# Order of the opening loads, and where the attention gate is computed, in an adaLN block with attention-like mixing and a lookup-table FFN

## What is computed

```python
mod = (silu(c) @ wmod).reshape(2, 6, 1, 512)
sa, ca, ga, sb, cb, gb = mod[:, 0], ..., mod[:, 5]
ga = (2 * (ga >= 0) - 1) * maximum(abs(ga), 0.25)        # "the gate"
h = layernorm(x) * (1 + ca) + sa
# attention part: project, rotate 64 features, relu, tanh, group norm, transpose
Q = relu(rope_rotate(h @ W_Q)); H = tanh(Q + hh_b)
out = group_norm_rows(H, gn_weight, gn_bias)             # 32 groups of 16 channels
x = x + ga * swapaxes(out, -2, -1).reshape(B, T, C)
# FFN part: weights are lut[idx], 16 values; gate, up (1376 x 512), down
h = layernorm(x) * (1 + cb) + sb
x = x + gb * ((silu(h @ Wg.T) * (h @ Wu.T)) @ Wd.T)
```

## Time and profile before

| | |
|---|---|
| median of 3 runs | 1066.49 us (1064.23 to 1067.11) |
| the profiled execution's own time | 1066.71 us |
| its span | 1064.9 us |
| TensorE busy | 962.3 us, 90% |
| VectorE, ScalarE, GpSimd busy | 597.5, 416.8, 170.2 us |
| mean granted TensorE clock | 0.958 |
| first projection starts | 46.11 us into the span |
| second projection starts | 89.40 us into the span |

### The profile page before, as it was taken

How to read it: one execution, slowest core, us unless ns; L and a number is a source line. 1 busy time by engine, 2 the same in 40 slices (tenths; PEclk the granted TensorE clock), 3 DMA queues, 4 the chain that set the end, 5 groups by cost and what they waited for, 6 DMA issues and landing times.

```text
span 1064.9 us, 13246 instructions
## 1 busy us (share of the span) xinstructions
PE 962.3 (90%) x4480; PEld 467.2 (44%) x4480; DVE 597.5 (56%) x1384; ACT 416.8 (39%) x626; POOL 170.2 (16%) x151
## 2 busy tenths in 40 slices
PE   5869569986888988999998989999999999999998
PEld 5534326434333433444444444444444444444443
DVE  5599995886588873333887876432222432222312
ACT  2365864458565642225543532331222422222200
POOL 3111202003466641112202200110000001000000
PEclk9989887988899999999999999999999999999999
DMA  8668363270101011234135114222000113000011
GB/s 291 218 172 217 74 182 71 68 238 1 38 22 30 20 56 73 79 109 119 34 124 145 35 57 147 81 79 89 0 0 0 51 40 109 0 0 0 1 40 40
DMA packets 33738, 83.91 MB, mean 79 GB/s; under 512 B 2976, under 2 KB 2976, under 8 KB 30368
## 3 DMA queue, kind: packets, MB, share of 16 engines
q1 hardware_dynamic: 32544, 75.00, 21.4%
q0 software_dynamic: 1152, 8.39, 4.2%
HBM read 64.50 MB, written 18.87 MB: 78 GB/s over the span
## 4 chain that ended last, share of the span: by engine, by line
PE 68%; DVE 16%; ACT 7%; issue 6%; DMA 2%; SPq 1%; POOL 1%; ACTq 0%; DVEq 0%
PE ps L1127 27%; PE ps L1161 22%; PE ps L1094 7%; PE ps L1116 4%; PE ps L1082 2%; DVE R L820 2%; PE ps L1139 2%; ACT w_all L532 2%; PE ps L1174 2%; DVE hid L798 1%; DMA w_all<-wmod_dram 1%; DVE hd L829 1%; ACT R L541 1%; PE ps L1106 1%; ACT h L480 1%
## 5 line engine op out<-in xcount | busy, mean ns | idle before, releaser
L1127 PE MATMUL ps<-h,w_all 128*128 128x512 f16 x1920 | 424.8, 383 | 19.1 <-DVE hd L829 16.4
L1127 PEld LDWEIGHTS ps<-h,w_all 128*128 (+1 forms) x1920 | 188.7, 99 | 252.6 <-issue 19.9
L1161 PE MATMUL ps<-w_all,hid 128*128 128x512 f16 x1056 | 231.2, 381 | 4.7 <-DVE w_all L1011 4.7
L1161 PEld LDWEIGHTS ps<-w_all,hid 128*128 128x128 f16 x1056 | 103.6, 98 | 129.6 <-DVE w_all L1011 5.2
L829 DVE SCALAR_TENSOR_TENSOR hd<-ps,col,sg 128x512 f32<-128x512 f32 x80 | 59.9, 749 | 149.3 <-ACT sg L502 149.3
L502 ACT ACTIVATE sg<-ps,col 128x512 f32<-128x512 f32 x80 | 54.6, 683 | 181.8 <-PE ps L1127 181.5
L854 DVE SCALAR_TENSOR_TENSOR hd<-ps,col,gbB 128x512 f32<-128x512 f32 x32 | 24.0, 751 | 148.4 <-PE ps L1161 148.2
L517 ACT ACTIVATE hid<-hd 128x512 f32 (+1 forms) x88 | 55.2, 630 | 113.4 <-DVE hd L829 100.2
L407 POOL TENSOR_TENSOR h<-h,h 128x512 f16<-128x512 f32 x32 | 37.2, 1183 | 389.5 <-ACT h L487 389.5
L1094 PE MATMUL ps<-WQ,work 128*128 128x512 f16 x384 | 89.1, 394 | 4.0 <-DVE col L944 3.1
L1116 PE MATMUL ps<-hid,w_all 128*128 128x512 f16 x352 | 87.8, 412 | 4.6 <-ACT w_all L532 4.6
(11 more groups left out here) (110 smaller groups left out, 833.8 us busy)
## 6 DMA issues: line engine op xcount, KB each, us to landing
R<-x_dram SPq DMA_DIRECT2D x16, 1024.0 KB, 6.6
xa<-x_dram SPq DMA_DIRECT2D x15, 1024.0 KB, 5.9
hid<-idx_dram SPq DMA_DIRECT2D x44, 256.0 KB, 6.9
R<-bias_dram POOLq DMA_DIRECT2D x8, 1024.0 KB, 8.1
out_dram<-R SPq DMA_DIRECT2D x32, 256.0 KB, 2.2
x_dram<-R SPq DMA_DIRECT2D x7, 1024.0 KB, 5.1
w_all<-wmod_dram SPq DMA_DIRECT2D x6, 1024.0 KB, 15.2
h<-idx_dram SPq DMA_DIRECT2D x11, 256.0 KB, 2.6
```

The source lines that it names most:

```text
L1127: ins = nc.tensor.matmul(bank(GU[2 * s + t]), W[wp][:, bass.ds(at, P)], h2[hp][:, s, k], start=(k == 0 and i == 0), stop=(k == K - 1 and i ...
L1161: ins = nc.tensor.matmul(bank(QY[par]), hid[hp][:, bass.ds(at, P)], W[wp][:, w_at:w_at + BLK], start=(j == 0 and i == 0), stop=(j == J - 1 ...
```

## The change

SyncE: the tokens of block 0 are loaded second and CA third, W_Q fourth; index chunk 1 moves behind the rotation tables. The store of the bias rows moves behind `load_idx(4)` of block 0. VectorE: `stats(0)` moves ahead of the wait for W_Q; SA and CA are copied to `vec` before the wait for `wq_all`; `masks(1)` and `gates_of_attn` move from ahead of the first rotation to behind the last `center` of block 0, and the last two `sum_squares` stay ahead of `masks(2)`. TensorE: GA's columns and rows are computed behind the first projection, and the wait for `row_ready` moves behind them, ahead of the first sum. ScalarE: `norm(0)` comes first; only chunk 0 is converted ahead of `affine(0)`; `make_bias(0)` and `half_idx(3)` move behind the tanhs and squares of block 0, ahead of `summed_out(0)`. Block 0 is written out ahead of the loops on TensorE and ScalarE. No product, transfer or vector step is added or removed.

```diff
--- before.py
+++ after.py
@@ -271,14 +271,14 @@
                 sp.dma_start(mod_w[s], mod_v[s]).then_inc(mod_in[s], 16)
 
             load_mod(SA)
+            load_x(x_toks[0, 0], 0)
+            load_mod(CA)
             sp.dma_start(wq_f32, wq.rearrange("(k p) n -> p k n", p=P)).then_inc(wq_in, 16)
-            load_mod(CA)
-            load_x(x_toks[0, 0], 0)
             load_idx(0, 0)
-            load_idx(1, 1)
             load_mod(GA)
             sp.dma_start(cosT[:], cos).then_inc(rope_in, 16)
             sp.dma_start(sinT[:], sin).then_inc(rope_in, 16)
+            load_idx(1, 1)
             load_rows(0, rows_of_block(0, 0))
             for s in (SB, CB, GB):
                 load_mod(s)
@@ -291,8 +291,6 @@
                 sp.dma_start(bias_dram[b], bias_rows[b]).then_inc(bias_out, 16)
 
             for q in range(NB):
-                if q == 0:
-                    store_bias(0)
                 if q + 1 < NB:
                     load_x(x_toks[0, q + 1], q + 1)
                     reach(sp, x2_out, 16 * q)
@@ -300,6 +298,8 @@
                 last = q == NB - 1
                 for w in range(AHEAD * (q + 1), AHEAD * (q + 2) - last):
                     load_idx(w, w % 2)
+                    if w == AHEAD:
+                        store_bias(0)
                 if last:
                     store_bias(1)
                 if not last:
@@ -553,26 +553,31 @@
                                                scale=gnb[:, k:k + 1])
                 ins.then_inc(bias_rows_ready, 1)
 
+            norm(0)
             act.wait_ge(lut_split, 1)
             half_idx(0, 0)
-            half_idx(1, 1)
-            norm(0)
             act.wait_ge(vec_ready, 1)
             affine(0, CA, SA, 0, hq[0], lambda: None)
-            act.wait_ge(row_ready, 1)
-            make_bias(0)
+            half_idx(1, 1)
             half_idx(2, 0)
 
-            def attn_block(q, last):
+            def attn_block(q, last, first=False):
                 w = AHEAD * q
                 tanh(q, 0)
-                half_idx(w + 3, 1)
+                if not first:
+                    half_idx(w + 3, 1)
                 tanh(q, 1); square(q, 0); tanh(q, 2); square(q, 1)
                 if not last:
                     norm(q + 1)
                 tanh(q, 3)
+                if first:
+                    square(q, 2); square(q, 3)
+                    act.wait_ge(row_ready, 1)
+                    make_bias(0)
+                    half_idx(w + 3, 1)
                 summed_out(w, 0)
-                square(q, 2); square(q, 3)
+                if not first:
+                    square(q, 2); square(q, 3)
                 if not last:
                     half_idx(w + 4, 0)
                 summed_out(w + 1, 1)
@@ -587,7 +592,8 @@
                 summed_out(w + 3, 1)
                 half_idx(w + 6, 0)
 
-            with act.Fori(0, NB - 1) as q:
+            attn_block(0, False, True)
+            with act.Fori(1, NB - 1) as q:
                 attn_block(q, False)
             make_bias(1)
             attn_block(NB - 1, True)
@@ -901,10 +907,15 @@
 
             wq_f32 = hid[0][:, 0:2 * K * C].bitcast(F32)
             wq_s = hid[1][:, 0:2 * K * C].bitcast(F32)
+            stats(0)
             dve.wait_ge(wq_in, 16)
             magnitude(wq_s, wq_f32)
             v.tensor_reduce(c_wqmax, wq_s, axis=AX, op=ALU.max).then_inc(wq_max, 1)
-            stats(0)
+
+            vps = bank(QY[1])[:, 0:5 * K * BATCH].rearrange("p (s k b) -> p s k b", s=5, k=K)
+            dve.wait_ge(vec_mm, 1)
+            v.tensor_copy(vec[:, SA], vps[:, SA])
+            v.tensor_scalar(vec[:, CA], vps[:, CA], 1.0, None, ALU.add).then_inc(vec_ready, 1)
             dve.wait_ge(wq_all, 1)
             exponent(c_e, c_wqall, 60, 186)
             field(c_sq, c_e, -1, 264)
@@ -916,8 +927,6 @@
                             ALU.subtract).then_inc(wq_ready, 1)
 
 
-            vps = bank(QY[1])[:, 0:5 * K * BATCH].rearrange("p (s k b) -> p s k b", s=5, k=K)
-
             gate_ps = bank(GU[3])[:, 0:5 * K * BATCH].rearrange("p (s k b) -> p s k b", s=5, k=K)
 
             def gate_of(dst, src, tmp, tmp2):
@@ -927,9 +936,6 @@
                 step(v.tensor_scalar(tmp2, tmp2, 0.25, None, ALU.max))
                 return v.scalar_tensor_tensor(dst, tmp, 1.0, tmp2, ALU.subtract, ALU.mult)
 
-            dve.wait_ge(vec_mm, 1)
-            v.tensor_copy(vec[:, SA], vps[:, SA])
-            v.tensor_scalar(vec[:, CA], vps[:, CA], 1.0, None, ALU.add).then_inc(vec_ready, 1)
             dve.wait_ge(rope_in, 32)
 
             def gates_of_attn():
@@ -946,7 +952,6 @@
 
 
             masks(0, 0)
-            gates_of_attn()
 
             def scales_of_ffn():
 
@@ -956,15 +961,21 @@
 
             def attn_block(q, half, last):
                 w = AHEAD * q
-                masks(w + 1, 1)
+                if q:
+                    masks(w + 1, 1)
                 rope_relu(q, q, 0); rope_relu(q, q, 1); center(q, 0); rope_relu(q, q, 2); center(q, 1)
                 if not last:
                     stats(q + 1)
                 rope_relu(q, q, 3)
                 sum_squares(q, 0); center(q, 2); sum_squares(q, 1); center(q, 3)
+                if q == 0:
+                    masks(w + 1, 1)
+                    gates_of_attn()
+                    sum_squares(q, 2); sum_squares(q, 3)
                 if not last:
                     masks(w + 2, 0)
-                sum_squares(q, 2); sum_squares(q, 3)
+                if q:
+                    sum_squares(q, 2); sum_squares(q, 3)
                 if last:
                     group_scale(q, 0)
                     masks(w + 2, 0)
@@ -1188,15 +1199,18 @@
             pe.wait_ge(silu_c, 1)
             pe.wait_ge(id_ready, 1)
             mod_vec((SA, CA))
-            mod_vec((GA,), GU[3])
             transpose_x(0, 0)
-            mod_row(GA, GU)
             pe.wait_ge(wq_ready, 1)
-            pe.wait_ge(diag_ready, 1)
-
-            def attn_block(q, last=False, scales=False):
+            pe.wait_ge(vec_ready, 1)
+
+            def attn_block(q, last=False, scales=False, gates=False):
                 w = AHEAD * q
                 project(q, q, 0)
+                if gates:
+                    mod_vec((GA,), GU[3])
+                    mod_row(GA, GU)
+                    pe.wait_ge(diag_ready, 1)
+                    pe.wait_ge(row_ready, 1)
                 sum_chunk(w, 0, True)
                 sum_chunk(w + 1, 1)
                 if last:
@@ -1211,8 +1225,8 @@
                 if not last:
                     transpose_g(q, q + 1)
 
-            pe.wait_ge(row_ready, 1)
-            with pe.Fori(0, NB - 2) as q:
+            attn_block(0, gates=True)
+            with pe.Fori(1, NB - 2) as q:
                 attn_block(q)
             attn_block(NB - 2, scales=True)
             pe.wait_ge(vec_ready, 2)
```

## The result

The forecast was 1068.0 us, between 1064.4 and 1071.4, the likeliest case no change. Measured: **1074.57 us** (median of 6, 1070.43 to 1080.12) against 1066.72 us for the kernel before (median of 6, 1064.23 to 1069.60), a ratio of 1.0071 with an interval of 1.005 to 1.0093. The change makes the kernel 7.9 us slower. The profiled execution took 1075.59 us, its span is 1073.8 us, 8.9 us more than before. The second projection starts at 93.28, just behind the 93 that the prediction gave as a sign of being wrong.

What follows compares the result with a forecast made beforehand. The gate and the loads ahead of it were taken to hold up the first projection. It starts 12.7 us earlier, but affine(1) comes +2.2, less 0.7 makes +1.5 us: 1068.0 us, range 1064.4 to 1071.4.

Steps and rivals of the forecast that it cites:

- the 93: Start of the second projection, forecast near 90.9; a start before 87 or after 93 would show the prediction wrong.
- The lower half of the operand: Block 0's operand before the first projection: first part due at 26.2, GpSimd busy until 27.0, 0.8 us delay, complete at 33.0.
- second rival: Opening: the reduction's idle time passes during GpSimd's wait; projection at 32.6, 0.8 us less, 1067.2 us; chance 0.17.
- Block 0: After the first projection: gate work behind VectorE's last centring puts row_ready at 65.2; some 20 us given back before the sums.
- The first sum: Behind row_ready in block 0: starts at 65.6, half rate for 4.5 us, done at 71.3, affine(1) 2.2 us later.
- took back 0.7: From affine(1) to the second projection: 2.5 us less at full rate, only 0.7 us credited, giving +1.5 us.
- What counts is how far 89.40 moves: From the second projection (89.40 before) both kernels run the same work, so its +1.5 us shift reaches the end unchanged.
- first rival: Half rate lasts through the first sum and returns at the transposes: +4.4 us, 1070.9 us; chance 0.20.

Runs made afterwards that it cites:

- lower_dve: Changed kernel with the lower half of block 0's operand written by VectorE instead of GpSimd; 1072.27 us, ratio 1.0055 to the kernel before.
- gate_only: Changed kernel with loads, statistics and SA and CA copies in the old order, gate still behind the projection; 1077.02 us, ratio 1.0089 to the kernel before.
- masks_front2: Changed kernel with the masks of chunk 1 back ahead of the rotations; 1071.35 us, ratio 1.0049 to the kernel before.
- gate_between: Changed kernel with the gate back ahead of the first attention block, behind the transposes, and masks(1) ahead of the rotations; 1058.05 us, ratio 0.9931 to the kernel before.
- after_third: Changed kernel traced a third time without an edit, one of the two repeats; 1072.45 us for one execution.
- after: The changed kernel itself in its first trace; median 1074.57 us, ratio 1.0071 to the kernel before.
- after_again: Changed kernel traced a second time without an edit, one of the two repeats; 1072.88 us for one execution.
- pool_early2: Changed kernel with one small GpSimd addition right behind the reduction; 1074.94 us, ratio 1.007 to the kernel before.

## Why the prediction was wrong

- **The lower half of the operand** ("where GpSimd is busy with the reduction until 27.0 ... 33.0") is the step that failed in the opening. GpSimd was done with the reduction at 22.91, as in my second rival: its idle time ran for the most part during the wait for the maximum. But ahead of the next ordinary instruction stands a second idle time, 6.87 to 7.77 us in the traces, which the kernel before hid behind ScalarE. The projection started at 36.15, 2.75 us late. A step moved from 34.68 to 26.2 had lost a cover that I had not named. By lower_dve an earlier projection alone would have gained 1.4 us at the first sum and 0.3 us at the second projection: index chunk 2, which no term of the sum has, and the idle time itself in block 1 take the rest.
- **Block 0** was right in mechanism and size: 31.2 us from the projection to `row_ready` against 31.8 forecast (32.6 and 32.7 in the two repeats). The mechanism, the gate standing behind VectorE's chain with the sums waiting for it, is what gate_only, masks_front2 and gate_between show.
- **The first sum** took 9.88 us with its fellow, 9.3 us forecast (65.6 to 74.9); `affine(1)` came 12.9 us after it, 12.2 forecast. From there to the second projection 13.00 us, 13.1 forecast. The pause of 2.96 us in it did not bring half rate at once: the transposes and sums took 2.1 us less than before, where the forecast took back 0.7. But the residual step behind masks that took 4.69 us kept TensorE waiting 1.4 us longer than before. That the two errors nearly cancel is luck. Up to the second projection the forecast is 2.4 us short (+3.9 in place of +1.5): 2.75 us from the late first projection, and -0.3 us from all other terms together.
- **"What counts is how far 89.40 moves"** is the second failed step. The second projection's own start ran at half rate, 0.54 over its first 3.7 us, which cost 1.7 us more (+3.9 became +5.6 at the third projection); in after_third it was the second pair of sums ahead of it instead (8.76 us in place of 7.07), with nearly the same total, +5.4 us. And the tail added 3.4 us in the profiled execution, 0.1 and 0.3 us in the two repeats. The forecast had no term for a later stage that runs the same work at another clock. In sum, for the profiled execution: 2.4 us in the opening, 1.7 us in the second projection and 3.4 us in the tail, over the forecast +1.5, give the +8.9 of its span within rounding.
- **The range** ended at 1071.4 us, 0.5 us above the first rival, so that it held one thing going wrong and not two. The measured opening, +5.5 to +6.5 us, has a second slow stretch, which is near the first rival though in another place (the transposes ran at full rate), and the late subtraction, which no rival had.

That the executions of the changed kernel spread over 9.7 us, and those before over 5.4 us, fits the tail, but how often each tail comes was not measured, and so the 1.4 to 2.4 us by which the medians differ more than the openings are put down to the tail by argument only.

## What to carry over

Work that only its own consumer needs is cheap to move into an idle stretch and expensive to move behind a chain: look first at which engine has a gap (in the changed kernel VectorE from 33.6 to 40.3, TensorE from 26.4 to 36.2), and put each part of the work there, rather than behind the step whose start one wants earlier. A wait on one engine in front of another engine's independent work, here `row_ready` ahead of the sums, turns all that stands ahead of the release into a part of the path, and the pause is paid a second time in TensorE's clock. When a step moves earlier, ask what its old wait was hiding on its own queue; and when an experiment takes such a cost away, look whether it comes back at the next instruction of the same kind.

## What the runs showed of the hardware that I had not expected

- Around `partition_all_reduce` GpSimd has two idle times, one ahead of it and one behind it, ahead of the next ordinary instruction. The first is 5.75 us before, where the input had long been ready, and 6.31 us after, where all but 1.96 us of it passed while the engine waited for the maximum (ready at 20.57, reduction at 22.53). The second is 6.87, 7.77, 7.05 and 7.63 us in after, after_again, after_third and pool_early2, and 9.87 us in lower_dve, where it came behind the accumulating transfer and 61 us after the reduction. The Trainium skill, "GPSIMD Engine Reference", section "Instruction dispatch", names a code load of about 6 us at the first call of a freshly loaded kernel, which agrees with the first. Of the second the page says nothing; the traces show how long it is and not what it is for.
- VectorE's eight masks take 2.77 us alone and 4.68 us (28.89 to 33.57) or 4.69 us (86.72) where GpSimd subtracts at the same time (29.78 to 32.27, 86.12 to 89.12). The Trainium skill, "SBUF — State Buffer", section "SBUF: two separate sides", has VectorE's two-port modes and GpSimd share one pair of ports as an exclusive lock; the two stretches agree with it.
- Full rate survived a pause of 2.96 us at 81.1 in the changed kernel and was gone after one of 3.10 us at 43.0 in the earlier trace rows. In after_again the transposes right behind one of 2.95 us ran at full rate (1.33 us for eight), and the first 4 us of the sums behind them at a granted clock of 0.57. The length of the pause alone does not tell.
